# Building the edge matrices: one of three weight multiplications goes from VectorE to GpSimd

## The reference, cut to what matters

```python
def _spmm(src, dst, w, x, n):
    return jax.ops.segment_sum(w[:, None] * x[src], dst, num_segments=n)
...
for W, b, g, be in ((W1, b1, g1, be1), (W2, b2, g2, be2)):
    agg = _spmm(src, dst, edge_weight, x, n)
    h = (x + agg) @ W + b
    x = jax.nn.gelu(_layer_norm(h, g, be), approximate=False)
```

## Time and profile before

| | |
|---|---|
| median of 3 runs | 1826.44 us (1825.96 to 1827.35) |
| span of the profiled execution | 1822.0 us |
| PE busy | 1704.3 us, 94% |
| PE weight load busy | 1363.7 us, 75% |
| DVE busy | 942.9 us, 52% |
| ACT busy | 569.8 us, 31% |
| POOL busy | 186.2 us, 10% |

### The profile page before, as it was taken

The page is one execution under the profiler, slowest core; times in us unless marked ns, Lnnn a source line. Parts: engine busy times, 40 slices in busy tenths (PEclk is TensorE's granted clock), DMA queues, the critical chain, the costliest instruction groups (busy, mean ns, idle before and its releaser), DMA issues.

```text
span 1822.0 us, 30852 instructions
## 1 busy us (share of the span) xinstructions
PE 1704.3 (94%) x10162; PEld 1363.7 (75%) x10163; DVE 942.9 (52%) x1593; ACT 569.8 (31%) x854; POOL 186.2 (10%) x260
## 2 busy tenths in 40 slices
PE   6999999888879999999999999999999999998995
PEld 4898988888766777777777777767677777787784
DVE  7999999998862300111144443552312243245436
ACT  2135677888880100000011111343400000004442
POOL 4000000000000100000000000000000000153683
PEclk9999999999999999999999999999999999999998
DMA  4203344544569445454443435900054434434375
GB/s 98 1 34 124 146 175 192 206 201 200 228 239 356 132 139 154 134 161 149 138 127 110 127 124 149 232 1 0 15 187 167 141 110 120 151 117 132 106 241 183
DMA packets 136919, 261.73 MB, mean 144 GB/s; under 512 B 22236, under 2 KB 74735, under 8 KB 136606
## 3 DMA queue, kind: packets, MB, share of 16 engines
q1 hardware_dynamic: 116824, 237.02, 40.2%
q0 software_dynamic: 5808, 14.70, 2.2%
q10 hardware_dynamic: 14230, 9.29, 1.7%
HBM read 161.13 MB, written 108.09 MB: 148 GB/s over the span
## 4 chain that ended last, share of the span: by engine, by line
issue 55%; PE 27%; ACT 6%; DVE 4%; ACTq 3%; DMA 2%; POOL 1%; DVEq 1%; SPq 0%; POOLq 0%
PE ps L2112 12%; PE ps L2113 4%; PE ps L2143 3%; ACT wide L870 3%; ACTq L914 2%; PE ps L2363 2%; ACT ps L818 2%; PE ps L2347 2%; DVE act_c L1373 1%; PE ps L2355 1%; PE ps L2339 1%; PE ps L2160 0%; ACTq L859 0%; DMA count_matrix<-wide 0%; PE ps L2015 0%
## 5 line engine op out<-in xcount | busy, mean ns | idle before, releaser
L2143 PE MATMUL ps<-wide 128*128 128x320 f32 (+1 forms) x2000 | 533.2, 427 | 0.0
L2143 PEld LDWEIGHTS ps<-wide 128*128 128x128 f32 x2000 | 378.4, 190 | 141.3 <-issue 0.4
L2112 PE MATMUL ps<-early,act_c 128*128 128x200 bf16 x2400 | 295.7, 252 | 43.4 <-issue 18.7
L2143 PE MATMUL ps<-wide,act_a 128*128 128x320 f32 (+1 forms) x1000 | 264.4, 426 | 2.3 <-DMA wide<-weight_matrix 2.2
L2112 PEld LDWEIGHTS ps<-early,act_c 128*128 128x128 bf16 x2400 | 220.5, 97 | 58.1 <-issue 57.3
L2143 PEld LDWEIGHTS ps<-wide,act_a 128*128 128x128 f32 x1000 | 189.8, 190 | 75.4 <-DMA wide<-weight_matrix 2.4
L870 ACT COPY wide<-ps 128x832 f32<-128x832 f32 x200 | 169.8, 849 | 121.8 <-PE ps L2113 120.6
L818 ACT ACTIVATE ps<-wide 128x832 f32 (+1 forms) x200 | 173.4, 868 | 42.0 <-ACT wide L870 33.7
L1373 DVE TENSOR_TENSOR act_c<-act_a,pair_tab 128x3072 bf16<-128x3072 bf16 x98 | 169.1, 1750 | 14.6 <-PE ps L2113 14.6
L1501 DVE TENSOR_TENSOR wide<-ps,rows 128x1280 f32<-128x1280 f32 x10 | 14.9, 1491 | 283.5 <-PE ps L2160 283.5
L2112 PE MATMUL ps<-act_a,act_c 128*128 128x200 bf16 x1152 | 140.3, 251 | 11.0 <-ACT ps L818 4.2
(11 more groups left out here) (261 smaller groups left out, 1808.5 us busy)
## 6 DMA issues: line engine op xcount, KB each, us to landing
wide<-weight_matrix SPq DMA_DIRECT2D x90, 800.0 KB, 4.5
wide<-count_matrix SPq DMA_DIRECT2D x45, 800.0 KB, 4.6
weight_matrix<-wide SPq DMA_DIRECT2D x60, 480.0 KB, 2.5
count_matrix<-wide SPq DMA_DIRECT2D x60, 480.0 KB, 2.6
weight_matrix<-wide SPq DMA_DIRECT2D x20, 560.0 KB, 2.7
count_matrix<-wide SPq DMA_DIRECT2D x20, 560.0 KB, 2.7
wide<-weight_matrix SPq DMA_DIRECT2D x20, 400.0 KB, 3.7
routed_tokens<-in_x_dram SPq DMA_DIRECT2D x2, 3072.0 KB, 30.4
```

The lines of the kernel that those rows point to most:

```text
L2112: nc.tensor.matmul(weights, hot_parts[:, slot % PART_SLOTS, part, two, :, k], hot_key[mask_slot][:, mask_two, 0:WCOLS, k], start=False, st ...
L2143: i = nc.tensor.matmul(ps[:, 2 * sub + h, 0:n], features[:, q * QUADS + t, h * P:(h + 1) * P], moving, start=q == 0 and t == 0, stop=q == ...
```

## The change

GpSimd gets a loop of its own for the build (lines 1167 to 1180 of the changed kernel). For every batch it waits for the half's `hot_lane` and for the batch three back to be used up, multiplies 1024 elements of `hot_lane` by the third weight part, and counts `thirds_made`. VectorE multiplies the first two parts only, so its operation becomes 128 x 2048 (line 1398). TensorE waits for `thirds_made` beside `batch_ready` ahead of each batch. Where TensorE and ScalarE wait against a register value, the value passes through a bitwise and with 2047 first, one more register instruction for each wait. VectorE waits once for the last third after the build. Elsewhere, two semaphores of the weight loads of the last mixture become one with the summed count, and the branch for unsorted edges, which does not run on this input, ends with counts that release GpSimd.

```diff
+        def weighed_by_pool(slot):
+            return True
+
+        def of_weights(step, slot, parts):
+            weights = pair_weight[:, ds(step * UNROLL + slot, 1), parts, :].rearrange("p g j (a k) -> p (g j) a k", k=2)
+            return weights.unsqueeze(3).broadcast_to([P, parts.stop - parts.start, TWOS, P, 2])
+
+        def of_lanes(half, b, parts):
+            return hot_lane[half][:, b * TWOS:(b + 1) * TWOS].unsqueeze(1).broadcast_to([P, parts.stop - parts.start, TWOS, P, 2])
...
-                    act.wait_ge(pair_done, end)
+                    act.wait_ge(pair_done, act.scalar_reg_alu(ALU.bitwise_and, end, COUNTED))
...
+            def third_parts(step, turns):
+                for half in range(turns):
+                    both_batches = step * MASK_SLOTS + half
+                    pool.wait_ge(lane_made, both_batches + 1)
+                    for b in range(MASK_BATCHES):
+                        slot = half * MASK_BATCHES + b
+                        if weighed_by_pool(slot):
+                            pool.wait_ge(pair_done, (both_batches + 2) * MASK_PAIRS + b * BATCH)
+                            third = slice(2, 3)
+                            pool.tensor_tensor(hot_parts[:, slot % PART_SLOTS, third], of_lanes(half, b, third), of_weights(step, slot, third), ALU.mult).then_inc(thirds_made, 1)
+
+            with pool.Fori(0, TURNS) as step:
+                third_parts(step, MASK_SLOTS)
+            third_parts(TURNS, TURNS_LEFT)
...
-                            dve.tensor_tensor(hot_parts[:, slot % PART_SLOTS], hot_lane[half][:, b * TWOS:(b + 1) * TWOS].unsqueeze(1).broadcast_to(weighed),
-                                              pair_weights.unsqueeze(3).broadcast_to(weighed), ALU.mult).then_inc(batch_ready, 1)
+                            dve.tensor_tensor(hot_parts[:, slot % PART_SLOTS, parts], of_lanes(half, b, parts), of_weights(step, slot, parts), ALU.mult).then_inc(batch_ready, 1)
...
+            dve.wait_ge(thirds_made, BATCHES)
...
-                            pe.wait_ge(acc_free, nc.s_assert_within(free, 1, WINDOWS // GROUP, skip_runtime_bounds_check_because="a group's number plus one"))
+                            pe.wait_ge(acc_free, pe.scalar_reg_alu(ALU.bitwise_and, free, COUNTED))
                             if half == 0:
                                 pe.wait_ge(batch_ready, step * UNROLL + batch + 1)
+                            if half == 0 and weighed_by_pool(batch):
+                                pe.wait_ge(thirds_made, step * UNROLL + batch + 1)
```

More of the change, by code:

```diff
@@ L75 @@
 UNROLL = MASK_SLOTS * MASK_BATCHES
+COUNTED = 2047
 BATCHES = -(-STEPS_P // MASK_PAIRS) * MASK_BATCHES
@@ L467, in build_program @@
         lane_made = sem("lane_made")
+        thirds_made = sem("thirds_made")
         batch_ready = sem("batch_ready")
@@ L504, in build_program @@
         gcn_in = sem("gcn_in")
-        moe_w1_loaded = sem("moe_w1_loaded")
-        moe_w2_loaded = sem("moe_w2_loaded")
+        moe_weights_loaded = sem("moe_weights_loaded")
         biases_loaded = sem("biases_loaded")
@@ L722, in _ @@
                         here_e = slice(e * D, (e + 1) * D)
-                        sp.dma_start(moe_w1[:, :, here_e], a["L1_ffn_w1"][e].rearrange("(k p) n -> p k n", p=P)).then_inc(moe_w1_loaded, 16)
-                        sp.dma_start(moe_w2[:, :, here_e], a["L1_ffn_w2"][e].rearrange("(k p) n -> p k n", p=P)).then_inc(moe_w2_loaded, 16)
+                        sp.dma_start(moe_w1[:, :, here_e], a["L1_ffn_w1"][e].rearrange("(k p) n -> p k n", p=P)).then_inc(moe_weights_loaded, 16)
+                        sp.dma_start(moe_w2[:, :, here_e], a["L1_ffn_w2"][e].rearrange("(k p) n -> p k n", p=P)).then_inc(moe_weights_loaded, 16)
                     sp.dma_start(moe_b1, a["L1_ffn_b1"].rearrange("e n -> (e n)").partition_broadcast(P)).then_inc(biases_loaded, 16)
@@ L1369, in one_hots @@
                             slot = half * MASK_BATCHES + b
-                            pair_weights = pair_weight[:, ds(step * UNROLL + slot, 1), :, :].rearrange("p g j (a k) -> p (g j) a k", k=2)
-                            weighed = [P, 3, TWOS, P, 2]
+                            parts = slice(0, 2 if weighed_by_pool(slot) else 3)
                             dve.wait_ge(pair_done, (both_batches + 2) * MASK_PAIRS + b * BATCH)
-                            dve.tensor_tensor(hot_parts[:, slot % PART_SLOTS], hot_lane[half][:, b * TWOS:(b + 1) * TWOS].unsqueeze(1).broadcast_to(weighed),
-                                              pair_weights.unsqueeze(3).broadcast_to(weighed), ALU.mult).then_inc(batch_ready, 1)
+                            dve.tensor_tensor(hot_parts[:, slot % PART_SLOTS, parts], of_lanes(half, b, parts), of_weights(step, slot, parts), ALU.mult).then_inc(batch_ready, 1)
                 with dve.Fori(0, TURNS) as step:
@@ L2092, in _ @@
                             pair(g, par)
+                pe.drain()
+                pe.sem_inc(pair_done, PPAD)
+                pe.sem_inc(lane_made, BATCHES // MASK_BATCHES)
             with pe.If(disordered < 1):
@@ L2322, in _ @@
             message_pass(2, [0])
-            pe.wait_ge(moe_w1_loaded, 16 * MOES)
-            pe.wait_ge(moe_w2_loaded, 16 * MOES)
+            pe.wait_ge(moe_weights_loaded, 16 * 2 * MOES)
             def experts_at(first, parts):
```

## The result

The changed kernel takes 1982.4 us (median of 4 runs, 1976.48 to 1988.71) against 1826.2 us (4 runs), a ratio of 1.086 with an interval of 1.0837 to 1.0889. The forecast was 2036 us with a range of 1960 to 2135, so the direction and the mechanism came true and the forecast was 54 us too long.

The account below looks back on a forecast made before the run. VectorE was taken to bound the build's first stretch. Its 5.29 us plus GpSimd's two multiplications made 9.55 us a half, times 74, starting streaming 210 us later: 2036 us, range 1960 to 2135.

Parts of the forecast that it names:

- What bounds the kernel: Build, before the change: VectorE full from 41 to 305 us at 6.35 us a half; afterwards no engine full, 7.0 us.
- VectorE's new work: Build: with each weighing cut from 3072 to 2048 elements, VectorE's own work a half falls from 6.35 to 5.29 us.
- Whether the engines run beside each other: Build: VectorE and GpSimd shut each other out for whole instructions, so their works add to 9.55 us a half.
- What it costs on GpSimd: Build: GpSimd's multiplication, scaled from an fp32 row, takes 2.23 us a batch, two batches a half.
- The hand-over's saving: Build: a shut-out instruction does some work ahead, saving GpSimd up to 0.20 us, so 2.03 to 2.23 us a batch.
- the end: Build's end to streaming: eight pairs on TensorE, 2.9 us, then 2.2 us, plus 0.6 us for first and last hand-overs.
- The rival of a quicker GpSimd: Build: GpSimd at the bf16 cast's pace, 1.55 us a batch, a half of 8.0 us, 1922 us in all; chance 0.12.
- Other engines under the pace: Build: TensorE's 5.76 and ScalarE's 6.4 us fit under 9.55 us a half, giving one pace in both stretches.
- The register instructions at nothing: Build: added register instructions on TensorE and ScalarE hide in waiting, costing 0; without that cover 0 to 27 us on TensorE.
- The first rival: Build: engines do run beside each other for bf16, TensorE bounds at some 6.0 us a half, 1812 us; chance 0.06.
- The clock: Build: TensorE drops to the low clock, 10.7 us a half, 85 us more if it stays, 2122 us; chance 0.06.
- the rival's last sentence: Build: a mixture of TensorE's two clock speeds would be mostly hidden, since TensorE has 3.8 us to spare.

Follow-up runs that it names:

- the write-only kernel: The changed kernel with GpSimd filling the third part by memset instead of multiplying, loop written out, third weight part left out of the result: 1849.4 us, ratio 1.010.

## Why the prediction was right, and where it was off

*What bounds the kernel.* VectorE's 6.35 us a half was right: the pace of 6.34 came back as soon as GpSimd stood aside and TensorE's sequencer was eased. VectorE's new work of 5.29 us was right as well: the paces with two and four multiplications, 8.69 and 12.08, give 1.70 us for one and 5.30 for VectorE, and with these the third, of one multiplication, comes out at 7.53 against 7.51 measured.

*Whether the engines run beside each other.* They do not, as the row of a copy stretched from 0.19 to 1.37 us said, and it holds for bf16: the 128-element operation grew from 0.22 to 1.91 us.

Of the two pages, the measurements bear out the Trainium skill's "SBUF — State Buffer", Who interferes with whom, in its finer point as well, that an instruction which only writes does not contend (the memset left VectorE's lengths alone). The note in the Trainium skill's "Advanced Engine Details and Errata", VectorE Performance Modes, which names only the two-port modes beside GpSimd, does not settle the question: a 16-bit `tensor_tensor`, which its table puts in the mode with one read port, was shut out all the same.

*What was mis-sized is "What it costs on GpSimd".* I scaled the fp32 row to 2.23 us a batch and took 2.03 to 2.23 us as held, 2.13 in the middle; the multiplication takes 1.89 us alone and holds 1.70. That is 0.43 us twice in 74 halves, 64 us too many. The hand-over's saving, 0.20 us, was read well (0.19). Against the 64 us stand 4.3 us by which I had the end too short: from the last half's end at 41.0 + 74 x 8.69 = 684.1 us to streaming at 694.1 are 10.0 us, where I put 5.7. I let eight pairs follow the last multiplication; TensorE took up its last sixteen at 683.33 us, ran the first of them at the low clock (0.67 us a pair until 686.5) and waited 0.84 us for ScalarE. So the build came out 59.4 us shorter than forecast (694.1 against 753.5). The part behind it was 4.1 us longer than before, where I had it unchanged, and the median stands 5.7 us above the span instead of 4.4: 59.4 less these 4.1 and 1.3 are the 54 us. The rival of a quicker GpSimd was the direction; I took its price from the cast, 1.55 us, where between the two rows would have been right.

*Other engines under the pace.* Right in both stretches: one pace of 8.69 us, and the slower halves of the second stretch slowed to it as well. The register instructions at nothing: right, shown by doubling them.

*The first rival's price was wrong*, though the rival did not occur. I let TensorE follow at 6.0 us a half, its array's 5.76 and some 0.24 for the table load, which takes 1.84. Without exclusion (the write-only kernel) a half took 6.3 to 7.0 us and the kernel was slower than before by 1.0%. Had I counted the sequencer's work (a load of 1.84 us, an estimated 0.25 us a pair, the added instructions), the shortest half would have come to about 6.1 us, and the gain to little.

*The clock.* The granted clock fell in the build, to 0.90 on average, and cost nothing but a part of the tail; the pace stayed 8.69 us in every half. That is the mixture that the rival's last sentence expected to be hidden. Its "once, at 440 us" was wrong: the clock of before also averaged 0.54 from 47 to 50 us, after TensorE had been busy for 0.09 of 2 us.

## What to carry to other kernels

Before giving a share of VectorE's `tensor_tensor` work to GpSimd, look for any row where a short instruction of the one is stretched beside a two-input instruction of the other; here the works simply add, so where VectorE is the bound a transfer pays only if GpSimd holds the reading for less time per element than VectorE would (1.66 against 0.52 ns here, from 1.70 and 0.53 us for 1024 elements), or if what it does reads no SBUF. And price the next bound by the engine's instruction stream as well as by its array: here halves bound by TensorE's sequencer took 6.27 us at the least, within 0.1 us of VectorE's 6.35.

## What the runs showed of the hardware that I had not expected

- A one-input copy of 1.03 us on GpSimd shuts out VectorE's two-input operations for 0.83 us; a memset of 0.95 us does not shut them out at all.
- A VectorE operation without a second tensor, 128x5 fp32 with a constant, was shut out as well: 3.90 us beside GpSimd's multiplications, 0.17 us otherwise. Five batch-norm statistics in a row beside the same multiplications kept their 1.7 us. What tells the two apart, and so whether two inputs on VectorE's side are needed at all, no experiment here settles.
- GpSimd's bf16 multiplication is shorter when one operand repeats along the columns (1.90 against 2.12 us for 1024 elements).
- Four register instructions a half on TensorE's sequencer, 32 to 39 ns each in the profile, go with 12 us in 74 halves (0.04 us each), and four more cost another 22 us, 0.07 us each.
